# A graph network's first table: low halves on GpSimd, later rows normalised on VectorE, and the first sixteen blocks placed ahead of the edge gathers

## What is computed

```python
x = x + gnn(layernorm(x), W1, b1, W2, b2, edges)        # edges = (src, dst)
x = x + soft_moe(layernorm(x)[None], phi, scale, w1, b1, w2, b2)[0]

def gcn_conv(x, W, b, src, dst, n):                     # src, dst with self-loops
    h = x @ W
    deg = segment_sum(ones, dst, n); dinv = rsqrt(deg)
    msgs = h[src] * (dinv[src] * dinv[dst])[:, None]
    return segment_sum(msgs, dst, n) + b
gnn: gcn_conv -> relu -> gcn_conv
```

## Time and profile before

| | |
|---|---|
| median of three runs | 3421.6 us |
| the profiled execution's own time | 3418.3 us |
| its span (first to last record) | 3416.5 us |
| TensorE busy | 3127.1 us, 92% |
| VectorE busy | 1949.8 us, 57% |
| GpSimd busy | 1831.5 us, 54% |
| ScalarE busy | 1206.3 us, 35% |
| end of `prepare`'s last low half | 213.4 us |
| first instruction of `first_layer` | 218.4 us |

### The profile page before, as it was taken

How to read it: one execution, slowest core, us unless ns; L and a number is a source line. 1 busy time by engine, 2 the same in 40 slices (tenths; PEclk the granted TensorE clock), 3 DMA queues, 4 the chain that set the end, 5 groups by cost and what they waited for, 6 DMA issues and landing times. The chain is left out here.

```text
span 3416.5 us, 56727 instructions
## 1 busy us (share of the span) xinstructions
PE 3127.1 (92%) x19474; PEld 2019.4 (59%) x19474; DVE 1949.8 (57%) x2989; ACT 1206.3 (35%) x1447; POOL 1831.5 (54%) x1754
## 2 busy tenths in 40 slices
PE   7229999999999999969999999999999997679998
PEld 7215666666666666635666666666666653245665
DVE  8774444444444444438777777787777773101333
ACT  6952232223232323215444444444444441111000
POOL 0137777777777777467666666666666631100000
PEclk9979999999999999979999999999999999799999
DMA  9499998999999999579998999899998977999996
GB/s 375 173 334 326 325 312 298 311 307 312 304 313 306 312 308 310 182 271 353 321 311 306 312 311 309 305 312 309 305 309 308 314 251 277 317 323 283 265 270 174
DMA packets 344440, 1018.61 MB, mean 298 GB/s; under 512 B 145314, under 2 KB 148668, under 8 KB 335984
## 3 DMA queue, kind: packets, MB, share of 16 engines
q0 software_dynamic: 135776, 660.85, 56.8%
q1 hardware_dynamic: 196916, 322.85, 28.8%
q10 hardware_dynamic: 11484, 31.39, 2.9%
HBM read 854.14 MB, written 135.08 MB: 290 GB/s over the span
## 5 line engine op out<-in xcount | busy, mean ns | idle before, releaser
L1266 POOL DMA_INDIRECT xs<-table,idx x833 | 881.3, 1058 | 481.9 <-PE m_part L1443 276.9
L816 POOL DMA_INDIRECT xs<-table,idx x833 | 901.2, 1082 | 345.4 <-issue 187.0
L1061 PE MATMUL a_part<-xs 128*128 128x512 f16 (+1 forms) x3332 | 584.2, 329 | 58.8 <-DMA xs<-table,idx 54.7
L1443 PE MATMUL m_part<-xs 128*128 128x512 f16 (+1 forms) x3332 | 586.5, 329 | 30.6 <-DMA xs<-table,idx 26.0
L1042 PE MATMUL a_ps_o<-Ws,xs 128*128 128x512 f16 x3528 | 591.1, 326 | 3.4 <-DVE xs L1020 2.0
L1061 PEld LDWEIGHTS a_part<-xs 128*128 128x128 f16 x3332 | 414.6, 142 | 189.0 <-issue 71.1
L1443 PEld LDWEIGHTS m_part<-xs 128*128 128x128 f16 x3332 | 418.3, 142 | 168.7 <-issue 47.1
L1042 PEld LDWEIGHTS a_ps_o<-Ws,xs 128*128 128x128 f16 x3528 | 345.6, 98 | 229.0 <-issue 2.8
L1471 PE MATMUL m_ps_l<-xs,m_xT 128*128 128x512 f16 x1764 | 388.7, 379 | 0.1
L1458 PE MATMUL m_ps_s<-m_dw,m_xn 128*128 128x512 f16 x1332 | 321.0, 380 | 3.7 <-DVE xs L1332 3.7
L1471 PEld LDWEIGHTS m_ps_l<-xs,m_xT 128*128 128x128 f16 x1764 | 172.2, 98 | 207.5 <-issue 1.6
(11 more groups left out here) (372 smaller groups left out, 3871.8 us busy)
## 6 DMA issues: line engine op xcount, KB each, us to landing
xs<-in_L_ffn_w_dram SPq DMA_DIRECT2D x64, 1152.0 KB, 10.0
xs<-table SPq DMA_DIRECT2D x98, 384.0 KB, 6.2
xs<-table,idx POOLq DMA_INDIRECT x1666, 5.1
cw_dram<-xs SPq DMA_DIRECT2D x49, 512.0 KB
x_pad<-xs SPq DMA_DIRECT2D x7, 2688.0 KB, 24.1
table<-arena SPq DMA_DIRECT2D x49, 384.0 KB, 4.6
table<-xs SPq DMA_DIRECT2D x49, 384.0 KB, 4.5
xs<-x_pad SPq DMA_DIRECT2D x49, 384.0 KB, 5.6
```

The source lines that it names most:

```text
L816: pool.indirect_dma_start(out=ring[:, t, :], out_offset=None, in_=table, in_offset=bass.IndirectOffsetOnAxis(ap=idx[:, k:k + 1], axis=0)). ...
L1061: mm = nc.tensor.matmul(part[:, bass.ds(to + a, z - a)], pick[:, i % 2, :, t], ring[:, t, half * D + a:half * D + z], start=False, stop=(t ...
L1266: pool.indirect_dma_start(out=ring[:, t, :], out_offset=None, in_=table, in_offset=bass.IndirectOffsetOnAxis(ap=idx[:, n:n + 1], axis=0)). ...
L1443: mm = nc.tensor.matmul(part[:, bass.ds(off + at, e - f)], pick[:, i % 2, :, t], ring[:, n % RING, half * D + f:half * D + e], start=False ...
```

## The change

- **Who normalises.** `by_scalar` is true for all of the blocks 0 to 15, and from 16 on for two of five (17, 19, 22, 24, ...): ScalarE 29 blocks, VectorE 20 instead of 7.
- **Who subtracts.** `low_by_pool` is true for blocks 0 to 15 and from 16 on for every third (16, 19, 22, ...): GpSimd makes 27 low halves, which it made none of; VectorE 22 instead of 49.
- **ScalarE's order.** AHEAD goes from 32 to 2: two blocks are normalised, and then a high half and a normalisation alternate.
- **GpSimd's order.** Low halves 0 to 15 stand ahead of the 14 gathers, the other 11 behind them.
- **VectorE's order.** Behind the plan it normalises its share six blocks ahead of the low half at hand; the two steps that turn the gathered tiles into `dloc` and `idx` come at blocks 26 and 32.
- **SP's order** is the same; it waits for the low half on the semaphore of the engine that makes it.

```diff
-        AHEAD = 32
+        AHEAD = 2
...
+        FRONT = 16
+
         def by_scalar(b):
-            return b % 7 != 6
...
+            return b < FRONT or (b - FRONT) % 5 in (1, 3)
+
+        def low_by_pool(b):
+            return b < FRONT or b % 3 == 1
...
                 for b in range(NBR):
                     sp.wait_ge(row_hi, b + 1)
-                    sp.wait_ge(row_lo, b + 1)
+                    low_made(sp, b)
...
+                def low_half(b):
+                    normalised(pool, b)
+                    pool.wait_ge(row_hi, b + 1)
+                    wait(pool, stored[b % TR], 16 * (b // TR))
+                    pool.tensor_tensor(stage[:, b % TR, D:2 * D], acc[:, b, :], stage[:, b % TR, 0:D], ALU.subtract).then_inc(row_lo_p, 1)
+
                 pool.wait_ge(iotas, 6)
+                for b in range(FRONT):
+                    low_half(b)
                 pool.wait_ge(steps_ready, 1)
...
+                for b in range(FRONT, NBR):
+                    if low_by_pool(b):
+                        low_half(b)
...
+                LEAD = 6
+                for b in range(FRONT, NBR):
+                    for q in range(FRONT if b == FRONT else b + LEAD - 1, b + LEAD):
+                        if q < NBR and not by_scalar(q):
+                            normalise(q)
+                    if b == 26:
+                        v.wait_ge(tiles_in, 16 * 2 * QC)
...
+                    if b == 32:
+                        v.wait_ge(tiles_t, 1)
...
+                    if not low_by_pool(b):
+                        low_half(b)
```

More of the change, by code:

```diff
@@ L298, in prepare @@
         row_lo = sem("t1_lo")
+        row_lo_p = sem("t1_lo_p")
         stored = [sem(f"t1_st{t}") for t in range(TR)]
@@ L303, in prepare, with normalised, low_made @@
         nround = (ET + 2 * HT - 1) // (2 * HT)
+        FRONT = 16
         def by_scalar(b):
-            return b % 7 != 6
-        def ys(b):
-            return sum(by_scalar(q) for q in range(b + 1))
+            return b < FRONT or (b - FRONT) % 5 in (1, 3)
+        def low_by_pool(b):
+            return b < FRONT or b % 3 == 1
+        def normalised(eng, b):
+            if by_scalar(b):
+                eng.wait_ge(y_ready, sum(by_scalar(q) for q in range(b + 1)))
+            else:
+                eng.wait_ge(own_y, sum(not by_scalar(q) for q in range(b + 1)))
+        def low_made(eng, b):
+            if low_by_pool(b):
+                eng.wait_ge(row_lo_p, sum(low_by_pool(q) for q in range(b + 1)))
+            else:
+                eng.wait_ge(row_lo, sum(not low_by_pool(q) for q in range(b + 1)))
         with nc.Block() as block:
@@ L398, in _ @@
                 for b in range(NBR):
[L399 to L402, removed]
+                    normalised(act, b)
                     wait(act, stored[b % TR], 16 * (b // TR))
@@ L626, in _, with low_half @@
                 link(v.tensor_scalar(bk128[:, :], s_id[:, :], float(P), None, ALU.mult))
[L628 to L636, removed]
+                def low_half(b):
+                    normalised(v, b)
+                    v.wait_ge(row_hi, b + 1)
+                    wait(v, stored[b % TR], 16 * (b // TR))
+                    v.tensor_tensor(stage[:, b % TR, D:2 * D], acc[:, b, :], stage[:, b % TR, 0:D], ALU.subtract).then_inc(row_lo, 1)
@@ L638, in normalise @@
                 def normalise(b):
-                    if b < NBR and not by_scalar(b):
-                        v.tensor_scalar(acc[:, b, :], acc[:, b, :], lnf[:, b:b + 1], lnb[:, b:b + 1], ALU.mult, ALU.add).then_inc(own_y, 1)
+                    v.tensor_scalar(acc[:, b, :], acc[:, b, :], lnf[:, b:b + 1], lnb[:, b:b + 1], ALU.mult, ALU.add).then_inc(own_y, 1)
                 v.wait_ge(factors, 1)
                 v.wait_ge(x_out, 16 * 7)
-                normalise(6)
-                normalise(13)
@@ L646, in _ @@
[L646 to L665, removed]
+                LEAD = 6
[5 more added lines that the diff above has]
+                        v.wait_ge(tiles_in, 16 * 2 * QC)
+                        for q in range(QC):
+                            last = v.tensor_scalar(work2[:, q, :], raw_dst[:, q, :], bk128[:, q:q + 1], None, ALU.subtract)
+                        last.then_inc(tiles_f, 1)
+                        v.tensor_copy(work[:, :, :], raw_src[:, :, :]).then_inc(tiles_f, 1)
+                    if b == 32:
+                        v.wait_ge(tiles_t, 1)
+                        v.tensor_copy(dloc[:, 0:NT], psT[:, 0:NT])
+                        v.tensor_copy(idx[:, :], psU[:, 0:NT])
+                    if not low_by_pool(b):
+                        low_half(b)
```

## The result

Median 3447.85 us in four runs (3447.09 to 3450.27), before 3422.51 in four; the ratio of the runs is 1.0081, 95% interval 1.0069 to 1.0094. The change makes the kernel slower by 25 us. The profiled execution took 3448.29 us, its span is 3446.2.

What follows compares the result with a forecast made beforehand. In `prepare` the plan's table, then ScalarE, then the DMA queues were taken to bound. Block 16 +18.8, rest 0, plan +7 gave +25.8 on 3418.3, plus 3.3 for the runs' median: 3447 us, range 3437 to 3460.

Steps and rivals of the forecast that it cites:

- No store before the plan's table, six blocks in front: Start of `prepare`: no store before 149.44 us and six ring slots, so six blocks get made beside the plan, not sixteen.
- Price of a low half, 1.8 us: One GpSimd subtraction: 1.8 us from three passes over 768 numbers at the iotas' rate, between 0.96 and 3.5.
- The ten blocks of the ring: Blocks 6 to 15, after store 0 lands: ten GpSimd low halves in a row, 153.2 to 171.2 us.
- The gathers, 18 us: The 14 gathers, now behind low half 15: 18 us instead of 20.5, ending at 189.2.
- Block 16: GpSimd's block behind the gathers: stored at 191.0 us instead of 172.2, +18.8 us, the main term, without the plan's delay.
- The plan's hold-up, +7: VectorE's serial chain up to `tab_ready`: six GpSimd subtractions beside it delay it by 7 us, bounds 0 and 10.8.
- rival A: Beside the plan: GpSimd and VectorE work side by side, no hold-up; +18.8 us, 3440; chance 27%.
- The two thirds: Share of the six subtractions' 10.8 us charged to the plan, since some steps read one tensor or PSUM or await TensorE.
- The rest, 0 with bounds -3.3 and +2.4: From store 16 to the last byte: 44.2 us before, taken as unchanged; ready blocks win up to 3.3, ScalarE's pace costs up to 2.4.
- The sum: Whole kernel: 18.8 + 0 + 7 = +25.8 us, giving 3447 us.
- `tiles_in` costs nothing: VectorE at block 26: the gathers land before it comes there, so this wait adds nothing; the stall covers it.
- rival C: `prepare`: sixteen blocks ready when SP gets to them, block 16 at about 165 us, 7 us early; 3413; chance 2%.

Runs made afterwards that it cites:

- Run 5: The changed kernel with SP's round trip of the plan's table moved from ahead of store 0 to behind stores 20 and 26: 3438.4 us, ratio 1.0052.
- Run 1: The changed kernel with the low halves of blocks 16, 19, 22, 25 and 28 on VectorE instead of GpSimd: 3437.5 us, ratio 1.0044.
- Run 6: The kernel before with six extra GpSimd subtractions beside the plan, on data that nobody uses: 3424.2 us, ratio 1.0013.
- Runs 2: The changed kernel with low halves 16 to 28 on VectorE and its tile steps moved from blocks 26 and 32 to 36 and 40: 3432.3 us.
- run 3: The changed kernel with all low halves from 16 on on VectorE and the tile steps at blocks 36 and 40: 3432.9 us, ratio 1.0038.

## Why the prediction was right

By its own steps:

- **No store before the plan's table, six blocks in front.** Right. The rows show six subtractions and a pause of 26.5 us. Run 5 shows the cause by taking it away: with SP's order changed the sixteen go through in one piece.
- **Price of a low half, 1.8 us.** 1.645 us where nothing holds it up (16.45 for ten). The estimate of 1.7 from the page (the Trainium skill, GPSIMD Engine Reference, section 3.1 Elementwise) was nearer than my three passes of the iotas.
- **The ten blocks of the ring.** Forecast from 153.2 to 171.2, without the hold-up. Measured from 159.35 to 175.80; less the 6.5 us by which the first store is late, that is from 152.9 to 169.3.
- **The gathers, 18 us.** 18.7 us; the last ten took 0.94 us each, most of them with VectorE standing.
- **Block 16.** Forecast 172.2 + 18.8 + 7 = 198.0, measured 196.40, 1.6 us earlier, mostly by the cheaper low halves. Run 1 shows that the gathers' place is the cause: with block 16 on another engine it goes at 177.39.
- **The plan's hold-up, +7.** 7.0 us at `tab_ready`, 6.5 at the first store. Run 6 reproduces it in the kernel before, so rival A (no hold-up) is refuted. The two thirds were right in size (7.0 of the 9.86 us that the six took) and only in part in reason: instructions that read PSUM or reduce do pass, but in run 6 a TENSOR_SCALAR of one tensor waited too (1.22 and 1.54 us).
- **The rest, 0 with bounds -3.3 and +2.4.** From store 16 to the first layer 47.9 us against 46.2: +1.7, within the bounds but not for the reason given. Behind block 16 the queues had 16.94 MB to move, 41.0 us at 413 GB/s and 43.0 with the 2 us from the last byte to the first layer; it took 4.9 us more. By my estimate from the stretches 1.8 of them are lost before 206 us, when the queues fill again after the pause (337 GB/s), 1.6 between 216 and 226, and 0.8 behind 236. In the last two VectorE sets the pace and not ScalarE, as the rows from 218 us on show. The prediction had VectorE at 1.04 us a block and waiting; it left out the tile steps and the normalisations' wait for GpSimd (1071 ns against 675). Runs 2 and 3 show that this wait is real and costs about what GpSimd's help brings. No run takes it out of the changed kernel itself, so VectorE's part in the 1.7 us is read from rows alone.
- **The sum.** +25.8 forecast, +25.9 at the first layer, +25.3 by the medians. The steps are right, but an agreement within 1 us is luck: block 16 came 1.6 us earlier than forecast and the rest took 1.7 us longer.

Of its signs, the wait for a store was given as about 20 us and took 26.5 (the prediction's own 153.2, with the 7 us of hold-up, less 134 gives 26), and the queues' share in the pause as 0.1 to 0.2, where it was 0.30.

No run takes away both the gathers' place and the plan's hold-up. Each is shown by itself, and how the 9.7 us that run 3 leaves are shared out is in part open.

Two things the prediction had too simple. It said that `tiles_in` costs nothing because the stall covers it; that is true as long as the stall is there, but run 1 shows a second wait of 8.3 us right behind it, so the two cannot be priced one by one: moving block 16 alone brought 7.3 of 18.8 us, with the tile steps 13.5. And rival C, "it does what its words say", was priced at 3413; run 5 met a condition that it names (a first store ahead of 125 us: 124.91) and came out 17 us slower than before at the first layer. C had left out that sixteen subtractions hold up the plan for 21.2 us, not for none, and so the gathers too.

## What to carry to other kernels

An instruction queue that issues DMAs in order is part of every producer's schedule: before work is moved ahead of something, follow the buffers it fills to the queue that empties them, and look what that queue waits for. When work is given to GpSimd, look at what stands behind it in the same list (here fourteen gathers, and a block behind the gathers) and count the VectorE instructions beside it as waiting. And when one stall is removed, expect the next wait for the same late thing: the first to come hides the others.

## What the runs showed of the hardware

VectorE and GpSimd exclude each other by what they read and write, and a short instruction can pay nearly the full length of the other. A VectorE instruction on 128x49 numbers took 1.62 us beside a GpSimd subtraction of 1.64. Beside GpSimd's memset, TENSOR_SCALAR instructions with a single tensor in SBUF took 1.50 and 1.79 us and instructions with two tensors 0.21. Beside a subtraction one that reads PSUM and one tensor took 0.21, and a TENSOR_REDUCE 0.25. A normalisation of 128x768 on VectorE took up to 2.06 us beside a subtraction instead of 0.67. Each subtraction beside the plan cost it 1.17 us (7.0 for six), and 1.33 (21.2 for sixteen) in run 5. The Trainium skill (SBUF — State Buffer, section Who interferes with whom) states just these two cases, single-input forms that use both ports and two-input forms that meet only GpSimd's reads; the trace agrees, with the durations above. In the other direction, GpSimd's gathers took 0.94 us beside an idle VectorE and up to 1.71 beside a busy one (run 3).
